# The opening stage of a four-layer chain is dissolved into the first steps of attention, and the engines get their own orders of steps at the transition

## The reference

```python
x = x + L0(x, cond)   # style = cond @ aff.T + b; w scaled by style and by rsqrt of its square sums;
                      # k = x w + b, q = k = v; scores of the 16 heads of ONE token (16 x 16), softmax,
                      # times v; then a second modulated linear layer (o)
x = x + L1(x, cond)   # U = cond @ W_dec (30 ranks of 512), weight = U @ V, x @ weight + bias
x = x + L2(x, cond)   # modulated linear layer, clipped to +-256
x = x + L3(x, ids, cond, ...)  # layer norms with rows gathered by ids, three small MLPs
                      # (memory, noise, resource: 2 rows each, 512 wide), concat of 6 blocks @ W1,
                      # silu, @ W2, layer norm
```

## Time and profile before

| | us |
|---|---|
| median of 3 runs | 1129.68 (1129.28 to 1135.8) |
| profiled execution, its own time | 1125.26 |
| its span, first to last instruction | 1123.4 |
| PE busy | 1040.6 (93% of the span) |
| POOL / DVE / ACT busy | 699.6 / 668.0 / 485.5 |
| mean granted TensorE clock | 0.964 |

### The profile page before, as it was taken

The page is one execution under the profiler, slowest core; times in us unless marked ns, Lnnn a source line. Parts: engine busy times, 40 slices in busy tenths (PEclk is TensorE's granted clock), DMA queues, the critical chain, the costliest instruction groups (busy, mean ns, idle before and its releaser), DMA issues.

```text
span 1123.4 us, 18260 instructions
## 1 busy us (share of the span) xinstructions
PE 1040.6 (93%) x6622; PEld 799.4 (71%) x6622; DVE 668.0 (59%) x1206; ACT 485.5 (43%) x755; POOL 699.6 (62%) x628
## 2 busy tenths in 40 slices
PE   8849999989999968499999999999999999999993
PEld 3536677766776646378888888788888888888872
DVE  2536776657667855476565665855655666555541
ACT  2028777766667652152333432423334233323330
POOL 1434565557564543557777776876877777776852
PEclk9779999989999989899999999999999999999997
DMA  7054546354322135221422423324132223313220
GB/s 268 1 158 133 180 136 239 118 192 142 123 95 74 50 123 215 89 82 49 132 79 69 141 68 100 138 82 127 69 106 95 93 80 106 106 58 115 69 67 19
DMA packets 55428, 123.21 MB, mean 110 GB/s; under 512 B 7567, under 2 KB 9745, under 8 KB 54304
## 3 DMA queue, kind: packets, MB, share of 16 engines
q1 hardware_dynamic: 43564, 80.11, 20.7%
q0 software_dynamic: 11776, 41.95, 11.9%
HBM read 104.09 MB, written 17.95 MB: 109 GB/s over the span
## 4 chain that ended last, share of the span: by engine, by line
PE 74%; DVE 6%; issue 5%; ACT 4%; POOL 3%; DMA 2%; POOLq 0%; SPq 0%; DVEq 0%; ACTq 0%
PE ps L759 38%; PE ps_k L804 7%; PE ps_y L766 7%; PE tp L771 5%; PE ps_o L766 5%; PE ps_s L795 2%; PE ps_v L831 2%; PE tp L960 2%; ACT at_diag L1044 1%; PE ps L1032 1%; PE ps_z L1021 1%; PE ps_u L820 1%; PE ps_vt L787 1%; PE ps_t L840 1%; ACT k_diag L1044 1%
## 5 line engine op out<-in xcount | busy, mean ns | idle before, releaser
L1578 POOL TENSOR_TENSOR rstd<-var_eps,half 128x1 f32<-128x1 f32 x96 | 54.2, 565 | 139.9 <-DVE var_eps L1420 139.2
L1537 POOL TENSOR_TENSOR om<-om,bc 128x512 f32<-128x512 f32 x32 | 46.3, 1446 | 85.7 <-DVE om L1302 85.7
L1168 ACT ACTIVATE g_out<-ps 128x512 f32<-128x512 f32 x32 | 19.2, 599 | 178.1 <-PE ps L1032 178.1
L1044 ACT ACTIVATE at_diag<-at 32x512 f32<-32x512 f32 x128 | 80.3, 627 | 27.2 <-PE ps_v L831 22.1
L1044 ACT ACTIVATE k_diag<-kt 32x512 f32<-32x512 f32 x128 | 80.0, 625 | 3.3 <-DVE kt L1283 2.2
L1426 DVE TENSOR_SCALAR shift_n<-mean_var,rstd 128x1 f32<-128x1 f32 x96 | 20.6, 214 | 94.1 <-POOL rstd L1578 92.1
L804 PE MATMUL ps_k<-wk_hi,xh 128*128 128x512 f32 x128 | 57.3, 447 | 17.6 <-DVE xl L1296 17.6
L1551 POOL TENSOR_TENSOR e<-e,rinv 128x512 f32<-128x512 f32 x32 | 33.6, 1050 | 60.4 <-DVE rinv L1267 60.4
L1406 DVE TENSOR_TENSOR t_lo<-tp,t_hi 128x512 fp32r<-128x512 f32 x64 | 43.8, 684 | 31.3 <-ACT t_hi L1138 31.3
L1142 ACT ACTIVATE h<-h,shift_n,rstd 128x512 f32<-128x512 f32 x32 | 26.1, 816 | 82.7 <-DVE shift_n L1426 82.7
L766 PE MATMUL ps_o<-oh,wo_hi 128*128 128x512 f32 x128 | 50.7, 396 | 8.1 <-DVE ol L1246 5.5
(11 more groups left out here) (256 smaller groups left out, 3268.3 us busy)
## 6 DMA issues: line engine op xcount, KB each, us to landing
raw<-in_dec_w SPq DMA_DIRECT2D x30, 512.0 KB, 5.7
x_in<-in_x_turned SPq DMA_DIRECT2D x32, 256.0 KB, 3.7
xb<-in_x_wide SPq DMA_DIRECT2D x32, 256.0 KB, 4.0
x_dram<-xb SPq DMA_DIRECT2D x32, 256.0 KB, 3.2
xt<-x_dram SPq DMA_DIRECT2D x8, 1024.0 KB, 8.3
out<-o SPq DMA_DIRECT2D x32, 256.0 KB, 2.0
raw<-in_int_W SPq DMA_DIRECT2D x7, 1024.0 KB, 6.2
w<-in_w_k_t SPq DMA_DIRECT2D x1, 1024.0 KB, 8.6
```

Source lines behind the costliest of these rows:

```text
L1044: last = nc.scalar.activation(dst[g, :, q, :], src[g, :, :], ACT.Copy)
L1537: nc.gpsimd.tensor_tensor(om[:, :], om[:, :], bc[:, STYLE_O, t // TB, :], ALU.mult).then_inc(om_ready, 1)
L1578: nc.gpsimd.tensor_tensor(rstd[:, k:k + 1], var_eps[:, k:k + 1], half[:, :], ALU.pow).then_inc(rstd_ready[k], 1)
```

## The change

The stage `opening` and its barrier are gone. Its work stands in `body`, in tiles that borrow room from buffers used later:

- SP issues cond, the k affine weight and its bias first, then the k weight in four pieces of 256 KB, then the first tile of x. All else of the opening follows. The first layer of the MLPs has its own piece of `raw[0]`, the second `raw[1:4]`.
- PE begins with the style of k alone; in prepare(-1) come the square sums of k; in prepare(0) the two spread rows of k and the first MLP layer; in prepare(1) the MLP turn, the style of o spread, the style of o; in prepare(2) the second MLP layer; in prepare(3) the square sums of o and a turn of table rows; in prepare(5) a second turn.
- The MLPs' three parts lie in three groups of 32 rows of one PSUM bank and of 96-row tiles, where before they were 2 rows by 1536; PE writes them with weights of 32 columns, in the order mem, noi, res for each slice.
- ACT and DVE split the k weight slice by slice ahead of their steps, and the o weight in prepare(4) and (5). POOL squares the k weight ahead of its steps, the o weight in prepare(1) and (2), and takes the powers in prepare(-1), (2) and (4).
- The U rounds begin at s = 5 and not 3; the side work behind them moves by two steps as a rule (styles of layer 2 to 6; loads to 16 to 27; table products to 20 to 29; the third sum of raw weights from 24 to 26). The eight fold products run without a gap at s = 26 to 33, the table's fold at 34 in place of 30, the copies of table parts (ACT) at 30 and 31 in place of 27 and 28. The product with w_2_t, r_rows, is at 18.
- `order` takes the engine. refine -5 to -3 are gone: lift, low rank and chunks of group 0 are steps of their own. ACT lifts group 0 before attend T+1, DVE within it, between two of its softmax operations. Group 1 is lifted before refine -1. PE and POOL do attend T+7 before refine -1, the others behind it; refine -2 remains for POOL and SP alone (gathers, the load of group 1), and SP does refine 0 before the splits. PE runs chunk (1, 0) at the head of refine 0, ahead of the turns. The last tile's high and low o parts come a step earlier (T+3).
- Semaphores of serial chains are merged (`softmax_step`, `k_step`, `mix_step`, `norm_step` and others count the links; `nth` gives the number). The merged waits name the events that they named before.

The list of steps:

```diff
 
-def order():
-
-    for s in range(-1, T):
+def order(engine):
+
+    for s in range(-1, T + 1):
         yield "attend", s
-    yield "attend", T
+    if engine == "ACT":
+        yield "lift", 0
     yield "attend", T + 1
-    yield "refine", -5
+    yield "low_rank", 0
     yield "attend", T + 2
-    yield "refine", -4
     yield "attend", T + 3
+    yield "chunk", 0
+    yield "attend", T + 4
+    if engine in ("POOL", "SP"):
+        yield "refine", -2
     yield "split", "x"
-    yield "refine", -3
-    yield "refine", -2
-    yield "attend", T + 4
+    yield "chunk", 1
+    yield "attend", T + 5
     yield "split", "t"
-    yield "attend", T + 5
+    yield "chunk", 2
+    yield "chunk", 3
+    yield "attend", T + 6
+    yield "lift", 1
+    if engine in ("PE", "POOL"):
+        yield "attend", T + 7
     yield "refine", -1
-    yield "attend", T + 6
-    yield "attend", T + 7
+    if engine not in ("PE", "POOL"):
+        yield "attend", T + 7
+    if engine == "SP":
+        yield "refine", 0
     yield "split", "s"
     yield "split", "h"
-    yield "refine", 0
+    if engine != "SP":
+        yield "refine", 0
     yield "split", "out"
```

SP ahead of its steps:

```diff
-            for t in range(2):
-                sp.dma_start(x_in[t][:, :, :], I["x_turned"][t]).then_inc(x_landed[t], 16)
+            sp.dma_start(cond[:, :, :], I["cond_t"].rearrange("(c p) b -> p c b", p=P)).then_inc(style_k_in, 16)
+            sp.dma_start(affs[0], I["aff_k_t"].rearrange("(c p) f -> p c f", p=P)).then_inc(style_k_in, 16)
+            sp.dma_start(aff_kbt[:, :, :], I["aff_bt"]).then_inc(style_k_in, 16)
+            for c in range(C):
+                sp.dma_start(w_raw[0][:, c, :], I["w_k_t"][c * P:(c + 1) * P, :]).then_inc(wk_in[c], 16)
+            sp.dma_start(x_in[0][:, :, :], I["x_turned"][0]).then_inc(x_landed[0], 16)
+            sp.dma_start(ident[:, :], I["ident"]).then_inc(consts_in, 16)
             sp.dma_start(at[0:2, 0:4, :].rearrange("p a b -> p (a b)"), I["mask_l"]).then_inc(consts_in, 16)
             sp.dma_start(e[0:2, :, :].rearrange("p a b -> p (a b)"), I["mask_r"]).then_inc(consts_in, 16)
             sp.dma_start(bias_k[:, :], row(I["k_b"], P)).then_inc(bias_in, 16)
+            sp.dma_start(x_in[1][:, :, :], I["x_turned"][1]).then_inc(x_landed[1], 16)
+            sp.dma_start(c64_wide[:, :], I["cond64_t"]).then_inc(mlp1_in, 16)
+            sp.dma_start(c32_wide[:, :], I["fside_t"]).then_inc(mlp1_in, 16)
+            sp.dma_start(mlp_w1[0], I["mem_W1"].rearrange("(c p) f -> p c f", p=P)).then_inc(mlp1_in, 16)
+            sp.dma_start(mlp_w1[1], I["noi_W1"]).then_inc(mlp1_in, 16)
+            sp.dma_start(mlp_w1[2], I["res_W1"]).then_inc(mlp1_in, 16)
+            for i, dst in enumerate((vec_b1, vec_b2, vec_g, vec_be)):
+                sp.dma_start(dst[0:MLP_ROWS, :], I["mlp_vectors"][i]).then_inc(vec_in, 16)
+            sp.dma_start(aw[:, :], row(I["aw"], P)).then_inc(vec_in, 16)
+            sp.dma_start(affs[1], I["aff_o_t"].rearrange("(c p) f -> p c f", p=P)).then_inc(aff_o_in, 16)
+            sp.dma_start(aff_ob[:, :], row(I["aff_o_b"], P)).then_inc(vec_in, 16)
             sp.dma_start(bias_o[:, :], I["o_b_t"]).then_inc(bias_in, 16)
+            for j, n in enumerate(MLPS):
+                sp.dma_start(mlp_w2[j][:, :, :], I[f"{n}_W2"].rearrange("(c p) f -> p c f", p=P)).then_inc(mlp2_in, 16)
+            sp.dma_start(w_raw[1][:, :, :], I["w_o_t"].rearrange("(c p) f -> p c f", p=P)).then_inc(wo_in, 16)
+            sp.dma_start(table_at[0:MLP_ROWS, :], I["table_rows"]).then_inc(wo_in, 16)
```

TensorE, ahead of its steps and in `prepare`:

```diff
+            pe.wait_ge(style_k_in, 16 * 3)
+            styles_turned(nc, ps_first[:, 0, :, :], affs[0], cond).then_inc(style_step, 1)
...
+                if s == -1:
+                    pe.wait_ge(style_step, 3)
+                    pe.wait_ge(square_ready[0], C)
+                    square_sums(nc, ps_squares[:, 0, :, :], w_sq[0], stsq_ko[:, 0, :, :]).then_inc(squares_step, 1)
+                if s == 0:
+                    pe.wait_ge(diag_ready, 1)
+                    nc.tensor.matmul(ps_diag[0], ones, diag_k[0], start=True, stop=True).then_inc(wide_mm, 1)
+                    pe.wait_ge(mlp1_in, 16 * 5)
+                    pe.wait_ge(cond_wide_ready, 1)
+                    for c in range(S // P):
+                        nc.tensor.matmul(ps_h[0:LOW, :], cond_wide[:, c, :], mlp_w1[0][:, c, :], start=c == 0, stop=c == S // P - 1)
+                    nc.tensor.matmul(ps_h[LOW:2 * LOW, :], c64_wide[:, :], mlp_w1[1], start=True, stop=True)
+                    nc.tensor.matmul(ps_h[2 * LOW:MLP_ROWS, :], c32_wide[:, :], mlp_w1[2], start=True, stop=True).then_inc(mlp_step, 1)
+                    pe.wait_ge(diag_ready, 2)
+                    nc.tensor.matmul(ps_diag[1], ones, diag_k[1], start=True, stop=True).then_inc(wide_mm, 1)
+                if s == 1:
+                    pe.wait_ge(mlp_step, 3)
+                    pe.wait_ge(consts_in, 16 * 3)
+                    turn_rows(mlp_h1, ps_h_t).then_inc(mlp_step, 1)
+                    pe.wait_ge(aff_o_in, 16)
+                    pe.wait_ge(cond_bc_ready, 2 * B)
+                    pe.wait_ge(demod_bc_ready, B)
+                    for b in range(B):
+                        for c in range(S // P):
+                            mm = nc.tensor.matmul(ps_style_o[b], cond_bc[:, c, b, :], affs[1][:, c, :], start=c == 0, stop=c == S // P - 1)
+                        mm.then_inc(style_o_mm, 1)
+                    pe.wait_ge(mlp_step, 5)
+                    styles_turned(nc, ps_first[:, 1, :, :], affs[1], cond).then_inc(style_step, 1)
+                if s == 2:
+                    pe.wait_ge(mlp2_in, 16 * 3)
+                    for c in range(C):
+                        for j in range(3):
+                            mm = nc.tensor.matmul(ps_h[LOW * j:LOW * j + LOW, :], mlp_t[:, c, LOW * j:LOW * j + LOW], mlp_w2[j][:, c, :],
+                                                  start=c == 0, stop=c == C - 1)
+                    mm.then_inc(mlp_step, 1)
+                if s == 3:
+                    pe.wait_ge(style_step, 6)
+                    pe.wait_ge(square_ready[1], C)
+                    square_sums(nc, ps_squares[:, 1, :, :], w_sq[1], stsq_ko[:, 1, :, :]).then_inc(squares_step, 1)
+                    pe.wait_ge(wo_in, 16 * 2)
+                    turn_rows(table_at, ps_rows_t).then_inc(rows_turned, 1)
+                if s == 5:
+                    pe.wait_ge(mlp_step, 14)
+                    pe.wait_ge(table_ready, 3)
+                    turn_rows(mlp_h2, ps_rows_t).then_inc(rows_turned, 1)
```

ScalarE, ahead of its steps and in `prepare`:

```diff
+            def split_high(j, c):
+                nc.scalar.activation((wk_hi, wo_hi)[j][:, c, :], w_raw[j][:, c, :], ACT.Copy).then_inc(wsplit_hi[j], 1)
+
+            for c in range(C):
+                act.wait_ge(wk_in[c], 16)
+                split_high(0, c)
...
+                if s == 0:
+                    for b in range(B):
+                        act.wait_ge(wide_mm, b + 1)
+                        nc.scalar.activation(bc[:, DEMOD_K, b, :], ps_diag[b], ACT.Copy).then_inc(demod_bc_ready, 1)
+                        if b == 0:
+                            act.wait_ge(mlp_step, 2)
+                            nc.scalar.activation(mlp_h1[0:MLP_ROWS, :], mlp_h1[0:MLP_ROWS, :], ACT.Silu).then_inc(mlp_step, 1)
+                    act.wait_ge(aw_step, 2)
+                    nc.scalar.activation(aw_exp[:, :], aw_low[:, :], ACT.Exp).then_inc(aw_step, 1)
+                if s in (4, 5):
+                    act.wait_ge(wo_in, 16 * 2)
+                    split_high(1, 2 * (s - 4))
```

VectorE, in `prepare(-1)`, `prepare(2)`, `prepare(26)` and in attend(T+1):

```diff
+                if s == -1:
+                    dve.wait_ge(consts_in, 16 * 3)
+                    nc.vector.tensor_copy(mask_lr[:, :], at[0:2, 0:4, :].rearrange("p a b -> p (a b)")).then_inc(mask_ready, 1)
+                    nc.vector.tensor_copy(mask_rr[:, :], e[0:2, :, :].rearrange("p a b -> p (a b)")).then_inc(mask_ready, 1)
+                    dve.wait_ge(squares_step, 1)
+                    nc.vector.tensor_scalar(vareps_ko[:, 0, :, :], ps_squares[:, 0, :, :], 1e-8, None, ALU.add).then_inc(squares_step, 1)
+                    for b in range(B):
+                        dve.wait_ge(demod_ready, b + 1)
+                        diagonals(nc, diag_k[b], ident, demod_t[:, 0, :, b]).then_inc(diag_ready, 1)
...
+                if s == 2:
+                    dve.wait_ge(mlp_step, 6)
+                    nc.vector.tensor_tensor(mlp_h2[m, :], ps_h[m, :], vec_b2[m, :], ALU.add).then_inc(mlp_step, 1)
...
+                    dve.wait_ge(demod2_step, 1)
+                    nc.vector.tensor_scalar(vareps[:, :, :], ps_demod, 1e-8, None, ALU.add).then_inc(demod2_step, 1)
+                if s == 26:
                     dve.wait_ge(tab_used, 4)
                     dve.wait_ge(x_sum_ready, 2)
                     nc.vector.scalar_tensor_tensor(flat(raw[0]), flat(raw[1]), wv[:, 4:5], flat(raw[0]), ALU.mult, ALU.add).then_inc(x_sum_ready, 1)
...
+                if s == T + 1:
```

(17 more changed lines are left out.)

953 lines of the change are left out of this document (447 added, 506 removed).

## The result

The changed kernel took 1092.74 us (1089.21 to 1094.99, 4 runs) against 1129.48 us: ratio 0.967, 95% interval 0.963 to 0.972. Measured again beside the last experiments it stood at 1091.86 us, ratio 0.968 (0.965 to 0.971). So it is 37 us faster, where the prediction said 47.5; 1092.7 lies within the range of 1063 to 1106, 10.7 us above the forecast. The profiled execution took 1093.44 us (span 1091.6), 31.8 us less than that of before; of the two profiled executions that of before lay 4.2 us under its median, that of after 0.7 above, which makes the 37 us.

What follows compares the result with a forecast made beforehand. PE was taken to set the time, except in the opening and the transition to the cascade. Opening -31.8, transition -18 and middle +2.3 sum to -47.5 us, so 1129.7 becomes 1082 us, range 1063 to 1106.

Steps and rivals of the forecast that it cites:

- First product: Opening: attention's first k product starts at 17.4 us (bounds 13 and 21) instead of 66.89, worth -49.5 us.
- The lock: Opening: DVE's k splits and POOL's k squares exclude each other; up to 2.3 us on the path, not in the sum.
- Returned work: Opening work that returns on PE in steps 0 to 5 of attention: +23.7 us (18.7 to 41).
- rival B: Opening: moved work stays in series and the clock low; PE's list costs 41 us, opening -14.5, total 1099; chance 0.16.
- The idle time to be filled: Steps 0 to 3: PE's idle 3.7 and 3.8 us take up 7.5 us of the returned work.
- the chain of step 0: Step 0: product 0's scale waits for square sums, a power, diagonals and a spread row with its copy: +3 us.
- The clock: Opening: at most one k product is left at low clock, where it costs 2.5 us more: -1.5 us.
- rival E: Attention: PE stays at 1.2 GHz, some 8 us more per step; six steps eat the 47.5, twelve give 1178; chance 0.03.
- Middle: Third raw sum on DVE now stands right ahead of constants the first fold product waits for: +2.3 us (0 to 4).
- Transition: Attention to cascade: PE's waits for DVE's remainder of x1 go and refine 0 begins earlier: -18 us (-6 to -25).
- rival C: Transition gives only the first wait, as the x3 chain stands bare on PE or x1 loads come late: -6, 1094; chance 0.11.
- I put it at 444: Transition: DVE's last x3 of group 0, done at 449.1 us before, would be done at 444.

Runs made afterwards that it cites:

- old_order: Changed kernel with all engines back on the one old list of steps, the opening still dissolved: 1107.34 us, ratio 0.983 to the kernel before.
- experiments 5 and 6: Kernel before with only the new orders of steps: 1111.21 us, ratio 0.985; changed kernel with the old list of steps: 1107.34 us, ratio 0.983.
- Experiment 3: Changed kernel with POOL's first three gathers (refine -2) moved behind attend T+7: 1087.68 us, ratio 0.967 to the kernel before.
- experiment 7: Changed kernel with the square sums of the o weight and of layer 2 cut from 16 passes to 4 each: 1079.85 us, ratio 0.958.
- gathers_late: The kernel of Experiment 3, the changed kernel with POOL's first three gathers behind attend T+7: 1087.68 us, ratio 0.967.

## Why the prediction was right in sign and size, and 10 us too low

The three terms are held against the profiled pair. There the sum said -47.5 and -32.0 came, 15.5 us less; the medians are 10.7 us off only because the two profiled executions lay at different places among their runs (4.2 below and 0.7 above). That much of the closeness is luck.

*First product.* Right: 16.82 us for 17.4. The style began at 5.15, the last quarter was squared by 9.9, the square sums took the 6.96 us of the low clock. The lock that I had left in the bound did not bite here: POOL's four squares took 4.21 us for 3.60, and DVE's splits of the k weight began only at 9.80.

*Returned work.* Right: 23.3 us for 23.7, summed from the timeline: spread rows 2.15, first MLP layer 3.8, its turn 0.5, style of o spread 3.8, style of o 3.6, second layer 3.56, square sums 4.63, turns of rows 1.3. The overlap of the MLPs' groups, which rival B doubted, is there: 24 passes in 3.56 us, for 10.46 in series at a partly lower clock.

*The idle time to be filled.* Too large. I let the returned work fill 7.5 us of idle time and gave back 3 for the chain of step 0. But PE idles 7.5 us from 17 to 107 (90 less 82.51) where it idled 9.1 in the same stage before: 1.6 less and not 4.5. Its old waits went and new ones came: 4.1 us for the MLP's turned rows behind x(2)'s late load, 3.0 for `k_diag`, ahead of which the chain runs through ACT and DVE with the split of the o weight.

*The clock, the term of the opening that failed.* "-1.5, since at most one k product is left at low clock." The clock was at the lower level for 0.17 x 2 x 90 = 30.6 us of this stage, where it had been 11.9 (0.09 x 2 x 66) before. PE's busy time grew by 25.6 us for 23.3 of returned work less a U round of 1.85; the remaining 4.2 us is old work at half the clock. I had the right mechanism in hand as rival E, and priced it as all or nothing: six steps at half clock or none. What came was its weak form, four short stretches. Together: opening -24.8 and not -31.8. Of the 7.0 the clock is 5.7 (4.2 and the -1.5 that didn't come), the idle time 2.9, and 1.7 come off for the work, the first product and steps 8 to 18. The five executions of this opening lie between -24.7 and -29.3, all short of the term; the nearest, old_order, is the one with the least half clock (0.10 x 2 x 84.6 = 17 us). So the size of the clock's part differs from one execution to the next, and the profiled one had much of it.

*Middle.* +5.4 for +2.3. The mechanism was the one named, the third sum ahead of the constants; its size was 3.8, at the upper end I had given, since POOL and the next step were held up as well. Of the rest, 1.6 us, the step from 32 to 33 has 0.7 (11.3 for 10.6), which goes with the new orders (experiments 5 and 6); what is left was not pulled apart.

*Transition.* -12.6 (-14.5 in the pair with the order alone) for -18, and not rival C's -6: both waits for the remainder of x1, 7.19 and 11.07 us, are gone from the list of PE's waits (the first low-rank product's weight load still waits 0.97). What failed is the sentence "I put it at 444", the end of x3 of group 0. Timeline of the kernel after, to be held against the earlier trace rows:

```profile
430.49 0.69 DVE L1457 TENSOR_TENSOR xt<-y,xt 128x512 f32<-128x512 f32 x1
...
435.82 0.60 PE L856 MATMUL tp<-ident,xt 128*128 128x128 f32 x4
...
447.64 0.80 PE L820 MATMUL ps_v<-z,v_parts 128*128 128x512 f32 x1 [9.38 <-DVE z L1471]
453.30 0.60 PE L856 MATMUL tp<-ident,xt 128*128 128x128 f32 x4
```

Counted from step 33 the last x3 was done 44.4 us on before and 45.9 us on after; I had it 5.1 us earlier. I followed PE's waits and left POOL's queue out, although its gathers were now ahead of two o biases. Experiment 3 showed it: with the gathers behind them the last x3 is done 40.2 us on, where I had it at 39.3, and 4.3 to 6.4 us come back. The rest of the term held: from the last x3 to the chunk at the head of refine 0 it took 16.5 us (15.5 forecast), with an idle PE for 9.38 (8 forecast).

*The marks I had set.* Right: first product 13 to 21, second layer under 4 us, no wait for `fl` above 2, one longer step at 26 (16.8 us for 11.5), under 12 us of idle PE ahead of refine 0. Wrong: fifth k product 66.95 (64), k products of 2.94 us only in some steps, refine 0 12.1 us earlier against step 33 (18 to 20). Of the things that were to prove the forecast wrong, the last came true: from 72 to 95 us other engines' queues were longer than PE's list.

## What to carry to other kernels

When idle stretches are filled with small pieces of work, price the clock of their neighbours too: taking out 7 us of narrow matmuls gained some 11 here, and at the place that could be told apart 3.5 us of them cost 1.6 to 3.9 us more in products behind them at half speed. When one engine is let through a wait, read the queues of the other engines at that place before the gain is booked; here three DMA issues on POOL took about a third of it. And a single trace of this kernel scatters by 5 us in its opening: compare stages over several kernels that share the code, and confirm small edits together.

## What was unexpected in the hardware

In the opening the granted clock fell four times before step 8 in each of the five executions of like code, each time during or right behind passes of 2 columns (at 60.8 and 94.8 us in the kernel after) or behind a wait of PE (at 36.9, in 4.1 us of idle time, and at 84.6, behind 1.9), but not for the same time. And not always: at 235 to 247 us, with the same code and the same 3.06 us of idle PE, the kernel after kept the upper level (its window stands with experiment 7), and old_order lost it:

```profile
235.00:247.00 12.00, 8.94 (x66) 5.94 (x65) 8.29 (x10) 6.74 (x13) 8.61 (x6) 0.86 0.48 161
```

The window of ten us from the stretch at 36.9 on, in the kernel after:

```profile
37.00:47.00 10.00, 9.54 (x59) 7.82 (x60) 4.02 (x11) 1.50 (x3) 1.84 (x2) 0.50 0.09 26
```

and in after_again, a second execution of the same kernel:

```profile
38.00:48.00 10.00, 10.00 (x66) 6.82 (x68) 4.27 (x11) 4.26 (x7) 1.67 (x3) 0.66 0.03 13
```

The five openings scatter by 5 us, and the shortest of them is the one with the highest granted clock (0.90 between 17 us and step 8, for 0.83 to 0.85). Idle products of 128 columns brought PE to the upper level by 7 us, where it came there at about 21 without them, and it was lost again during the passes of 2 columns that followed. And the issue of a gather on POOL, 1.21 and 0.94 us in the kernel before, took 2.47 and 1.45 us with 2.28 us of idle time ahead of it in the kernel after, and 1.21 and 0.94 again in gathers_late. It is not constant in the rest either (2.87 and 1.97 us in gathers_late at the next tile), and no run shows what it depends on.
